# Normalising four tiles at once with a broadcast operand, or tile by tile with a per-partition scalar, in a fused latent-attention network

## The reference, cut to what matters

```python
def _layernorm(x, axis=-1, eps=1e-05):
    m = jnp.mean(x, axis=axis, keepdims=True)
    v = jnp.var(x, axis=axis, keepdims=True)
    return (x - m) / jnp.sqrt(v + eps)

x = x + _L0_xattn_ref(ctx_1024, _layernorm(x, axis=-1), ...)   # cross attention, 16 heads of 64
x = x + _L0_attn_ref(_layernorm(x, axis=-1), ...)              # gated recurrence
x = x + _L0_ffn_ref(_layernorm(x, axis=-1), ...)               # low-rank experts, top 2
x = x + _L1_xattn_ref(_layernorm(x, axis=-1), ctx_1024, ...)   # cross attention, 1 head
x = x + _L1_attn_ref(_layernorm(x, axis=-1), ...)              # linear attention
x = x + _L1_ffn_ref(_layernorm(x, axis=-1), ...)               # causal attention and experts
x = x + _L2_xattn_ref(ctx_1024, _layernorm(x, axis=-1), ...)   # cross attention, 8 heads of 64
x = x + _L2_attn_ref(_layernorm(x, axis=-1), ...)              # local attention
x = x + _L2_ffn_ref(_layernorm(x, axis=-1), ...)               # 8 experts with a capacity
x = x + _L3_xattn_ref(_layernorm(x, axis=-1), ctx_1024, ...)
x = x + _L3_attn_ref(_layernorm(x, axis=-1), ...)              # state-space block
x = x + _L3_ffn_ref(_layernorm(x, axis=-1), ...)               # 8 experts, top 1
```

## Time and profile before

| | |
|---|---|
| median of 3 runs | 2430.18 us (2424.86 to 2434.6) |
| the profiled execution, its own time | 2427.39 us |
| its span in the profile | 2425.6 us |
| granted TensorE clock, mean | 0.991 of full speed |
| PE busy | 2312.0 us, 95% |
| DVE busy | 1490.3 us, 61%, 4040 instructions |
| ACT busy | 1163.5 us, 48% |
| POOL busy | 916.8 us, 38%, 853 instructions |

### The profile page before, as it was taken

The page is one execution under the profiler, slowest core; times in us unless marked ns, Lnnn a source line. Parts: engine busy times, 40 slices in busy tenths (PEclk is TensorE's granted clock), DMA queues, the critical chain, the costliest instruction groups (busy, mean ns, idle before and its releaser), DMA issues.

```text
span 2425.6 us, 41921 instructions
## 1 busy us (share of the span) xinstructions
PE 2312.0 (95%) x16426; PEld 1567.8 (65%) x16426; DVE 1490.3 (61%) x4040; ACT 1163.5 (48%) x2998; POOL 916.8 (38%) x853
## 2 busy tenths in 40 slices
PE   9999989999989999999999999999999999999998
PEld 6766656666766665666666675666666666666665
DVE  6457566666575567666564567756665555665653
ACT  5544334555445533445644453545555445354543
POOL 5334353433234336434332444543323243544310
PEclk9999999999999999999999999999999999999999
DMA  5000000000000000000000000000000000000000
GB/s 235 1 1 1 1 14 1 10 1 27 1 1 1 1 1 10 18 10 1 19 1 1 1 1 5 10 14 10 10 5 1 1 1 1 1 1 1 2 1 14
DMA packets 6821, 26.57 MB, mean 11 GB/s; under 512 B 864, under 2 KB 992, under 8 KB 5984
## 3 DMA queue, kind: packets, MB, share of 16 engines
q1 hardware_dynamic: 6624, 23.89, 2.7%
HBM read 21.79 MB, written 2.10 MB: 10 GB/s over the span
## 4 chain that ended last, share of the span: by engine, by line
PE 75%; DVE 16%; issue 3%; ACT 3%; POOL 3%; DMA 0%; POOLq 0%; DVEq 0%; SPq 0%
PE ps L486 9%; PE ps L499 8%; PE ps L549 7%; PE ps L518 6%; PE ps L510 4%; PE ps L889 4%; PE ps L628 4%; PE ps L603 3%; PE ps L471 3%; PE ps L596 3%; PE ps L650 3%; PE ps L601 3%; PE ps L677 2%; PE ps L846 2%; DVE P L1405 2%
## 5 line engine op out<-in xcount | busy, mean ns | idle before, releaser
L1919 POOL TENSOR_TENSOR P<-P,small 128x384 f32<-128x384 f32 x384 | 316.1, 845 | 564.0 <-DVE small L1430 564.0
L1140 ACT ACTIVATE P<-ps,small 128x192 f32<-128x192 f32 x768 | 315.0, 425 | 134.3 <-DVE small L1422 132.8
L1892 POOL TENSOR_TENSOR small<-small,mhalf 128x4 f32<-128x4 f32 x112 | 126.5, 1130 | 511.9 <-DVE small L1410 255.2
L499 PE MATMUL ps<-kvT,big 128*128 128x192 f32 x1536 | 311.4, 333 | 4.5 <-DVE big L1439 1.8
L499 PEld LDWEIGHTS ps<-kvT,big 128*128 128x128 f32 x1536 | 248.8, 190 | 74.9 <-issue 45.1
L1422 DVE TENSOR_REDUCE small<-ps 128x2 f32<-128x384 f32 x384 | 208.3, 550 | 108.8 <-PE ps L499 100.4
L486 PEld LDWEIGHTS ps<-wts,P 128*128 128x128 f32 x1920 | 232.3, 192 | 45.3 <-issue 30.6
L486 PE MATMUL ps<-wts,P 128*128 128x128 f32 x1920 | 247.8, 278 | 3.8 <-DVE P L1827 2.1
L2009 POOL TENSOR_TENSOR P<-T 128x512 f32<-128x512 f32 x96 | 125.4, 1306 | 197.2 <-DVE T L1709 128.2
L518 PEld LDWEIGHTS ps<-value,big 128*128 128x128 f32 x1536 | 178.6, 192 | 28.3 <-issue 18.6
L518 PE MATMUL ps<-value,big 128*128 128x128 f32 x1536 | 188.0, 278 | 0.1
(11 more groups left out here) (287 smaller groups left out, 4495.6 us busy)
## 6 DMA issues: line engine op xcount, KB each, us to landing
ctok<-ctok_dram SPq DMA_DIRECT2D x8, 512.0 KB, 4.1
ctxT<-ctx_dram SPq DMA_DIRECT2D x8, 512.0 KB, 4.1
wts<-weights_dram SPq DMA_DIRECT2D x1, 2530.0 KB, 23.3
wts<-weights_dram SPq DMA_DIRECT2D x1, 2189.0 KB, 17.8
X<-x_dram SPq DMA_DIRECT2D x8, 256.0 KB, 3.5
big<-fold_dram SPq DMA_DIRECT2D x2, 1024.0 KB, 8.5
out_dram<-X SPq DMA_DIRECT2D x8, 256.0 KB, 2.3
wts<-weights_dram SPq DMA_DIRECT2D x1, 1536.0 KB, 25.8
```

What stands on the lines that cost most here:

```text
L499: m = pe.matmul(ps[s][:, at:at + KEYS], big[s][:, BANK * b + 128 * p:BANK * b + 128 * p + 128], kvT[s][:, keys_at(b):keys_at(b) + KEYS], s ...
L1140: m = act.activation(probs(s, b // 2)[:, to:to + KEYS], ps[s][:, at:at + KEYS], ACT.Exp, bias=small[s][:, 4 * e + p:4 * e + p + 1], accum_ ...
L1892: pool.tensor_tensor(rstd(s, name, n), variance(s, name, n), mhalf[:, 0:n], ALU.pow).then_inc(*sig("rstd", s))
L1919: m = pool.tensor_tensor(view, view, over(small[s][:, at:at + 2], 2, [128, 2, KEYS]), ALU.mult)
```

## The change

Both functions issue four instructions of 128 columns (`tensor_scalar`, the tile's mean or reciprocal deviation as a scalar for each partition, read from SBUF) where one `tensor_tensor` of 512 columns read the statistics through a broadcast view. `m` is the last of the four, and it alone signals. Nothing else of the program and nothing of the written orders is changed.

```diff
                 def centre(s, name, dst, src):
-                    link(dve.tensor_tensor(by_tile(dst), by_tile(src), mean_var(s, name)[:, :, 0:1].to_broadcast([128, TILES, D]),
-                                           ALU.subtract))
+                    for t in range(TILES):
+                        m = dve.tensor_scalar(tile_of(dst, t), tile_of(src, t), mean(s, name, t), None, ALU.subtract)
+                    link(m)
 
                 def rescale(s, i, name, dst, src):
                     yield
                     dve.wait_ge(*on("rstd", s, i, name))
-                    dve.tensor_tensor(by_tile(dst), by_tile(src), over(rstd(s, name), 2, [128, TILES, D]), ALU.mult).then_inc(*sig("tok", s))
+                    for t in range(TILES):
+                        m = dve.tensor_scalar(tile_of(dst, t), tile_of(src, t), rs(s, name, t), None, ALU.mult)
+                    m.then_inc(*sig("tok", s))
```

## The result

The changed kernel takes 2467.03 us (median of 6 runs, 2460.81 to 2469.9), the kernel before 2431.23 us (6 runs): a ratio of 1.0166, 95% interval 1.0149 to 1.0183. That is 36 us slower. The forecast was 2444 us, and 2467 lies above the range of 2425 to 2462. The profiled execution took 2467.66 us, with a span of 2465.8 us.

A forecast was written before the change was run, and what follows sets the result against it. PE was taken to bound the kernel, busy 2312.0 of 2425.6 us. Added waits of 8.2 + 12.5 - 2.6 = 18.1 us, three quarters counted as 13.6, on 2430.2 gave 2444 us, range 2425 to 2462.

The forecast's parts named there:

- The price of four: On DVE: four pieces take 0.88 us undisturbed, so a rescale grows by 0.19 us and a centre by 0.20.
- The cheap scalar: Rival, on DVE: the four take 0.69 us, as much as now, and only gaps add; 2438 us, chance 0.10.
- the one-port rate: Rival, on DVE: the pieces take 1.13 us but never wait for POOL; 2424 us, not slower, chance 0.14.
- the 508 ns of the estimate: On DVE, from the skill's page: four take 508 ns against 594 for one, saving 0.09 us each.
- What PE sees of it: At 43 rescales PE already waits for, 0.19 us each: +8.2 us; the other 53 cost 0.
- The gaps: POOL instructions get in between the four rescale pieces at 19 places, 11 of them awaited by PE: +12.5 us.
- The rival that POOL never gets between: Rival, on DVE: the second piece claims its place before the first lets go, so no gaps; 2434 us, chance 0.18.
- What comes back: POOL's power slips in behind the centre's first piece, so rescales in 16 norms start up to 0.37 us sooner: -2.6 us.
- The sum of waits: Added PE waits from instruction time, gaps and the earlier power: 8.2 + 12.5 - 2.6 = 18.1 us.
- The step that failed: From PE's added waits to the kernel's end: three quarters of 18.1 us count, as later waits get shorter: +13.6 us.
- PE's busy time is unchanged: On PE: the change adds nothing to its busy time of 2312.0 us.
- The queue rival: Rival: longer rescales and gaps hold all of DVE and delay its other work, +25 us; 2455 us, chance 0.16.

The follow-up runs named there:

- The `tensor_tensor` pieces: Rescale and centre in four pieces as in the change, but as `tensor_tensor` with a broadcast statistic: 1.0163 against the kernel before, 2465.61 us.
- the small delay: Kernel before, rescale whole, then a 128-column reduction of a spare tile that signals in its place, results some 0.2 us later: 1.0047, 2438.06 us.
- the large delay: Kernel before, rescale whole, then a 512-column reduction of a spare tile that signals in its place, results some 0.6 us later: 1.0194, 2477.19 us.
- the fillers: Four constant matmuls before PE's wait for the rescale, nine norms: 1.0066 (2444.65 us) in the kernel before, 1.0159 (2468.35 us) in the changed one.
- the combination: Against the kernel before: centre in four, nine rescales in one-port pieces, six of them with four signals, three rescales whole: 0.9940, 2412.44 us.

## Why the prediction was wrong

**The price of four: the number right, the reason not.** I took 0.88 us, from L1488 less the faster rate of a single SBUF source; measured 0.87. The cheap scalar (0.69), the one-port rate (1.13) and the 508 ns of the estimate are all out: a piece takes 0.28 us, and the next starts 0.196 us behind it. But the faster rate isn't what makes L1488's 0.34 into 0.28. The `tensor_tensor` pieces take 0.28 too, though against the centre's 683 ns for 512 columns they run at (683 - 284) / 384 = 1.04 ns for a column, the rate of L1488. So that the term came out at 0.88 is partly luck.

**What PE sees of it: right.** +8.2 us forecast, +8.5 measured alone by the small delay, in one profiled execution.

**The gaps: right in kind, somewhat low where PE waits.** I forecast 19 places and 19.5 us over all of them. In the trace after, 20 of the 96 sets have a second, third or fourth piece longer than 0.35 us, 24 such pieces, together 22.6 us over the undisturbed 0.28. Of the places where PE waits I forecast 11 and 12.5 us; 15 sets that PE's loads wait for have such a piece, 17.1 us in all, and of PE's idle time the gaps make 15.3 us by the difference to the small delay. The rival that POOL never gets between is out. The Trainium skill's rule (SBUF — State Buffer, "Who interferes with whom") is that whoever issues first has the shared ports for its whole instruction while the other stands still. The third piece above agrees: it took 2.02 us in place of 0.28, beside the 2.05 us of L1936.

**What comes back: small, as forecast.** With the rescale in four, idle is 3.5 us lower with the centre in four than without (133.9 against 137.4; forecast 2.6); with the rescale whole it is 1.4 us higher (115.0 against 113.6). In the time it can't be told from zero.

**The sum of waits: right.** 18.1 us forecast, 20.3 measured as PE's whole added idle time; the waits of its loads for the rescale grew by 74.9 - 58.5 = 16.4.

**The step that failed** is the one from PE's waits to the end of the kernel: "Not all reaches the end ... I take three quarters, a choice between 0.5 and 1". The factor is not below 1: it was 40.2 / 20.3 = 2.0 in the profiled executions, and 35.8 / 20.3 = 1.8 by the medians. Two things were wrong in it. Later waits gave nothing back: all of PE's idle time grew by 20.3 us, no less than the waits for the rescale. This alone would have left the forecast inside its range, at 2430.2 + 18.1 = 2448 us. The larger one is a term that I had put at nothing without a reason, "PE's busy time is unchanged": it rose by 19.9 us, from stretches at 1.2 GHz. I had the granted clock of 0.991 in my table and never asked what stood behind the missing 0.9%. That a factor of 2 turns my 18.1 us into 2467 us is fitted afterwards, and no forecast.

How sure is this? That the busy time rose is a reading, and that it rose by the clock follows from the 20.1 us that the granted clock accounts for. That added waits bring the lower clock is shown by the large delay, which adds nothing but waiting (clock 0.984 to 0.985 in all four executions, 0.986 to 0.992 before), only weakly by the small one, and by the fillers, which take half of the waits for the rescale away (from 51 to 30 for PE's loads, in the changed kernel) and shrink the loss from 35.8 to 23.7 us. Which wait brings it is open: at one place 3.11 us did in one run and didn't in another. The share isn't fixed either: with the rescale alone it was 23.8 us idle and 12.2 busy at the same total. The queue rival's 2455 us was nearer in time than my forecast, for a reason that isn't there.

## What to carry to other kernels

When an engine's wait is at the edge of a saturated TensorE, price the wait and then look at the granted clock of the whole run: here each microsecond of added idle time cost between 0.4 us (the delays) and 1 us (the changed kernel) more at the lower clock. Splitting an instruction that can't run beside another engine's costs the instruction overhead, 0.19 us here for four pieces, and the other engine's next instruction wherever one is ready at a seam; count the places where that engine has two instructions queued. Pieces that don't meet the other engine cost nothing in total here, though they were slower, since they no longer waited for it. A signal for each piece gave back about half of the loss in the changed kernel (1.0166 to 1.0088); only the combination beat the kernel before.

## What the runs showed of the hardware that I had not expected

- A wait of 3.11 us of PE was followed by 10 us at a granted clock of 0.51; at the same place a wait of 1.25 us was followed by ten at 1.00, and so was a wait of 3.11 us in the run with only the rescale in four.
- Waiting in small slices between transposes brought PE's idle time back by 20 us but the clock only from 0.983 to 0.986.
- POOL's power over 4 columns took a mean of 1130 ns with the centre as one DVE instruction of 512 columns, and 1025 ns with the centre as four of 128. That it slips in at a seam, as POOL's longer instructions do, is the likely reason; no row of a single place is shown for it.
- `scalar_tensor_tensor` pieces with one operand in SBUF and one in PSUM were never held by POOL: 0.34 us at the median and 0.35 at the longest, over 288 pieces, where `tensor_scalar` pieces from SBUF were held for up to 2.1 us.
